# Attention gather in two halves of the TensorE array, with a zero-one product that repeats the parts

## The chip, the core and the metric

The kernel runs on one core of one Trainium2 chip. The metric is device time in microseconds (us) of one execution; several executions are timed and the median is given.

## The reference

One block with two batches of 2048 tokens of width 256, in float32. Only the attention matters here, and of it this:

```python
q, k, v = (split_heads(h @ W + b) for W, b in ...)      # 16 heads of width 16
scores = einsum('bhqd,bhkd->bhqk', q, k) * scale
sparsity = scores.max(-1) - scores.mean(-1)
_, top_idx = top_k(sparsity, U)                         # U = 307 of 2048 queries, per head
q_sel = take_along_axis(q, top_idx[..., None], axis=2)
attn = softmax(einsum('bhud,bhkd->bhuk', q_sel, k) * scale)
out_sel = einsum('bhuk,bhkd->bhud', attn, v)            # scattered back into zeros, then @ Wo
```

The block also has a layer norm ahead of the attention, and after it a second layer norm and a soft mixture of 8 experts.

## The kernel before

The program writes out the order of every engine by hand, with semaphores between the engines. For each batch it makes q, k and v, finds the maximum of the scores of every query (`maxima`, L1080 on VectorE), ranks the queries (`select`), and then runs `attend(b)`, the part that is changed, once for each batch. After both, the experts run.

`attend(b)` goes through 16 heads. To keep float32 accuracy on bf16 matmuls, q and k stand as three bf16 parts each, and a score is a sum of six products of parts. So the stationary and moving operands of a score have 6 * 16 = 96 rows (`TERMS`), of which the query parts are repeated as 0, 0, 0, 1, 1, 2, and 3 more rows with the negated maximum in three parts; 2 further rows carry the query's index. For head h the steps are these.

- **SK and OH** (VectorE, `build` and `onehot`). `SK` holds, for each of the 16 tiles of 128 tokens, 101 columns: the six copies of parts (L1224, six copies), the maximum's parts (L1225) and the index (L1260, once). `OH` is a zero-one matrix, 128 x 307 for each tile, with a one where a token has rank r (L1215, 16 instructions). Both have two buffers.
- **gather** (TensorE, L1666): 16 matmuls, one for each token tile, 101 stationary columns, 307 moving columns, all accumulated in PSUM bank 4. They pick the 307 chosen queries, already turned. They are cut in three pieces (`CUTS`, L1708: tiles 0 to 4, 5 to 10, 11 to 15). For head h the first piece stands at the end of head h - 2 and the other two within head h - 1.
- **take_queries** (ScalarE, L744) copies the 101 rows from PSUM to `QS` in bf16.
- **scores** (TensorE, L1678): 8 steps k = 0 to 7 of two matmuls each, into banks 0 and 1 for even k, 2 and 3 for odd k.
- **exps** (ScalarE, L752): for each step one exponential of 128 x 614 from PSUM to one of four slots of `PX`.
- **values** (TensorE, L1689): 4 steps of four float32 products (each is two matmuls in the trace), each of the four in its own 32-column group of the array.
- **rows** (L1697, three matmuls of one moving column) gives the indices, **turn** (L1704, three transposes) turns the output of the head before, and VectorE (`finish`, L1240 to L1244) divides; POOL scatters the result to DRAM (L609).
- **keys**: SyncE loads the keys of head h + 2 (`attention_keys`, L429) once the scores of head h are done, into one of two buffers `K2S`.

`pe_head` (L1710) sets TensorE's order within a head: for k4 = 0, 1, 2 come scores 2*k4+2 and 2*k4+3, values k4, then for k4 = 0 and 1 a piece of the next head's gather, and for k4 = 2 `rows` and `turn`; then scores 0 and 1 of the next head, values 3, and the first gather piece of the head after the next. `act_head` sets ScalarE's order: exps 0 to 6, take_queries of the next head, exps 7.

The waits that matter: score step k waits on `p_ready` until exps k - 2 has emptied its banks; values k4 waits for exps 2*k4+1; score step 0 of a head waits for `take_queries` of that head; a new gather into bank 4 waits for `take_queries` of the gather before. ScalarE executes strictly in the order written. In the second batch, ScalarE also has a square (L790) after the exps of most heads.

At the start of `attend`, POOL fills pads (`pads`, L580 to L585); the last ones wait for the ranking, and VectorE starts `build` of head 0 only when they are done (L1255).

## Time and profile before

| | us |
|---|---|
| median of 3 runs | 1721.07 |
| the runs | 1720.02 to 1728.72 |
| the profiled execution, its own time | 1707.33 |
| its span, first to last instruction | 1705.2 |

The profile is of one execution, whose own time is 2.1 us above its span and 13.7 us (0.8%) below the median of the runs. The attention stages are about 509 to 637 us and 1016 to 1148 us of the span; the rest is the preparation of each batch (with the maxima) and the experts. In the views, PE is TensorE's matmuls, PEld its weight loads, DVE is VectorE, ACT ScalarE, POOL GpSimd, and SPq SyncE's DMA queue. "a<-b" reads: output a, input b. "issue" as a releaser means that the profile shows nothing that was waited for. A matmul's duration runs from its start to its last result; matmuls overlap, so their pitch is shorter than that.

### The profile page before, as it was taken

How to read it: one execution, taken by the hardware profiler on the slowest of the kernel's cores; microseconds unless marked ns; L12 is line 12 of the kernel's file. 1: busy time of each engine (PE TensorE's matmuls, PEld its weight loads, DVE VectorE, ACT ScalarE, POOL GpSimd, SP SyncE). 2: the span in 40 equal slices, each digit the busy share in tenths (PEclk: the TensorE clock that was granted, in tenths of full speed). 3: DMA queues.
4: the chain of work that ended last, by engine and by line, in shares of the span. 5: the costliest groups of instructions: out<-in, count | busy, mean ns of one | idle time of the engine just before them, and what ended most of it. 6: DMA issues, size and time to landing. Idle time of an engine off the chain costs nothing.

```text
span 1705.2 us, 28768 instructions
## 1 busy us (share of the span) xinstructions
PE 1511.2 (89%) x8650; PEld 846.4 (50%) x8650; DVE 1243.7 (73%) x2937; ACT 1031.6 (60%) x1380; POOL 302.4 (18%) x363
## 2 busy tenths in 40 slices
PE   2779999998859998999999769999899999989999
PEld 1342222222435542222222545543588987469988
DVE  3659999999767858999999777876755452665511
ACT  2338888887736667888888426773333374334364
POOL 1370000000733445000000223442111100011100
PEclk7889999999979999999999879999999999999999
DMA  9441111112331120111112201111034302004410
GB/s 239 178 130 34 41 37 49 44 37 74 121 101 47 52 72 26 48 45 37 41 50 76 62 26 46 52 40 62 13 102 158 126 32 80 0 25 157 157 47 31
DMA packets 91789, 119.25 MB, mean 70 GB/s; under 512 B 21346, under 2 KB 77378, under 8 KB 91204
## 3 DMA queue, kind: packets, MB, share of 16 engines
q1 hardware_dynamic: 88644, 117.73, 22.9%
q0 software_dynamic: 3072, 0.66, 0.4%
q8 instruction: 32, 0.52, 0.1%
q14 instruction: 41, 0.34, 0.1%
HBM read 93.54 MB, written 24.78 MB: 69 GB/s over the span
## 4 chain that ended last, share of the span: by engine, by line
PE 42%; DVE 32%; issue 13%; DMA 5%; ACT 4%; SPq 2%; POOL 1%; PEld 0%; DVEq 0%; ACTq 0%; PEldq 0%; POOLq 0%
DVE work_area L1080 23%; PE psum L1884 6%; PE psum L1822 6%; PE psum L1666 4%; PE psum L1689 4%; PE psum L1765 4%; PE psum L1678 3%; PE psum L1833 3%; PE psum L1842 3%; DVE big_area L1080 2%; PE psum L1525 2%; DMA work_area<-heads_out 2%; PE psum L1874 2%; DVE work_area L1161 1%; ACT big_area L800 1%
## 5 line engine op out<-in xcount | busy, mean ns | idle before, releaser
L1080 DVE CUSTOM_DVE_ANT_0 work_area<-psum,work_area 128x1024 f32<-128x1024 f32 x512 | 589.6, 1220 | 18.4 <-PE psum L1572 14.6
L734 ACT ACTIVATE work_area<-psum 128x1024 f32<-128x1024 f32 x512 | 510.9, 1027 | 88.8 <-DVE big_area L1080 33.1
L1572 PE MATMUL psum<-work_area 96*128 96x512 bf16 x1024 | 312.0, 387 | 47.9 <-DVE big_area L1080 7.6
L1562 PE MATMUL psum<-work_area 96*128 96x512 bf16 x1024 | 309.7, 385 | 12.8 <-DMA work_area<-q_parts 6.8
L752 ACT ACTIVATE work_area<-psum 128x614 f32<-128x614 f32 x256 | 164.1, 681 | 79.4 <-PE psum L1678 78.8
L1572 PEld LDWEIGHTS psum<-work_area 96*128 96x128 bf16 x1024 | 64.4, 98 | 267.3 <-DVE big_area L1080 249.2
L1562 PEld LDWEIGHTS psum<-work_area 96*128 96x128 bf16 x1024 | 89.9, 98 | 161.0 <-ACT work_area L734 57.6
L609 POOL DMA_INDIRECT heads_out<-work_area x96 | 99.1, 1032 | 145.7 <-DVE work_area L1244 124.4
L1215 DVE TENSOR_SCALAR big_area<-iota,rank 128x308 bf16<-128x308 f16 x512 | 122.0, 312 | 0.0
L1822 PE MATMUL psum<-work_area,xn 128*128 128x128 f32 x1024 | 117.3, 275 | 0.0
L1765 PE MATMUL psum<-slots_T,work_area 128*128 128x512 f32 x256 | 116.6, 599 | 0.0
L1884 PE MATMUL psum<-expert_out,work_area 128*128 128x256 f32 x512 | 115.6, 379 | 1.1 <-ACT work_area L865 1.1
L1822 PEld LDWEIGHTS psum<-work_area,xn 128*128 128x128 f32 x1024 | 116.0, 192 | 0.2
L1666 PE MATMUL psum<-big_area,work_area 128*101 128x307 bf16 x512 | 91.4, 315 | 24.4 <-DVE big_area L1215 24.4
L570 POOL CAST negmax_parts<-negmax 128x256 bf16<-128x256 f32 x2 | 1.2, 615 | 577.1 <-DVE sparsity L1148 577.1
L1884 PEld LDWEIGHTS psum<-expert_out,work_area 128*128 128x128 f32 x512 | 95.1, 190 | 13.1 <-ACT work_area L865 1.3
L1666 PEld LDWEIGHTS psum<-big_area,work_area 128*101 128x101 bf16 x512 | 60.7, 133 | 72.5 <-issue 68.6
L1678 PE MATMUL psum<-work_area 99*128 99x307 bf16 x512 | 90.8, 297 | 5.5 <-ACT work_area L752 2.2
L1689 PE MATMUL psum<-work_area 128*32 128x307 f32 x1024 | 93.6, 438 | 0.0
L1421 DVE SCALAR_TENSOR_TENSOR work_area<-psum,rz,x_res 128x256 f32<-128x256 f32 x32 | 15.5, 483 | 98.1 <-PE psum L1884 59.8
L800 ACT ACTIVATE big_area<-psum 128x1024 f32 (+1 forms) x32 | 32.8, 1024 | 88.6 <-PE psum L1765 88.6
L635 POOL TENSOR_TENSOR work_area<-big_area,work_area 128x1024 f32 (+1 forms) x16 | 39.4, 2465 | 205.8 <-PE psum L1826 182.3
(236 smaller groups left out, 1994.4 us busy)
## 6 DMA issues: line engine op xcount, KB each, us to landing
work_area<-in_L_ffn_w_dram SPq DMA_DIRECT2D x32, 1024.0 KB, 5.4
work_area<-q_parts SPq DMA_DIRECT2D x192, 64.0 KB
k_parts<-work_area SPq DMA_DIRECT2D x24, 384.0 KB, 3.2
work_area<-k_parts SPq DMA_DIRECT2D x32, 192.8 KB
q_parts<-work_area SPq DMA_DIRECT2D x16, 384.0 KB, 2.5
big_area<-q_parts SPq DMA_DIRECT2D x16, 384.0 KB, 7.3
work_area<-k_parts SPq DMA_DIRECT2D x32, 192.0 KB
work_area<-k_parts SPq DMA_DIRECT2D x32, 128.5 KB
```

The source lines that it names most:

```text
L734: s.activation(SC[:, t % 4], PS[:, 2 * (n % 2):2 * (n % 2) + 2].rearrange("p a n -> p (a n)"), ACT.Relu).then_inc(relu_done, 1)
L752: s.activation(PX[:, slot, :, 0:U], PS[:, 2 * (k % 2):2 * (k % 2) + 2, 0:U], ACT.Exp, scale=SCALE).then_inc(p_ready, 1)
L1080: v.tensor_tensor_reduce(SC[:, t % 4], PS[:, 4 + 2 * (t % 2):6 + 2 * (t % 2)].rearrange("p a n -> p (a n)"), SC[:, t % 4], 1.0, -3.0e38, A ...
L1215: last = v.tensor_scalar(OH[:, par, t], iota[:], rank[:, t, bass.ds(h, 1)], None, ALU.is_equal)
L1562: last = mm(PS[:, 2 * (n % 2) + k], QS1[par][0:TERMS, t * P:(t + 1) * P], KS[par][0:TERMS, k * 512:(k + 1) * 512], start=True, stop=True)
L1572: last = mm(PS[:, 4 + 2 * (t % 2) + k], QS1[par][0:TERMS, t * P:(t + 1) * P], KS[par][0:TERMS, K1 + k * 512:K1 + (k + 1) * 512], start=Tru ...
L1666: last = mm(PS[0:TERMS + 5, 4, 0:U], SK[:, n % 2, t, 0:TERMS + 5], OH[:, n % 2, t, 0:U], start=(t == 0), stop=(t == NT - 1), skip_group_ch ...
L1678: last = mm(PS[:, 2 * (k % 2) + kk, 0:U], K2S[n % 2][0:TERMS + 3, kt * P:(kt + 1) * P], QS[0:TERMS + 3, n % 2, 0:U], start=True, stop=True)
L1689: last = mm(PS[32 * q:32 * q + 32, 6 - n % 2, 0:U], Vh[:, n % 2, kt], PX[:, kt // 2 % 4, kt % 2, 0:U], start=(kt < 4), stop=(kt >= NT - 4) ...
L1765: last = mm(PS[:, 2 + 2 * par + k], XT[:, par, cc], SNT[:, cc, k * 512:(k + 1) * 512], start=(cc == 0), stop=(cc == DC - 1))
L1822: last = mm(PS[:, cc, 0:P], XN[:, t, cc * P:(cc + 1) * P], E1[:, t], start=(t == 0), stop=(t == NT - 1))
L1884: last = mm(PS[:, 5 - par, 0:D], E2T[:, par, e], EO[:, e], start=(e == 0), stop=(e == E - 1))
```

## The change

The gather's stationary operand `SK` shrinks from 101 used columns to 53 (three parts of 16, three of the maximum, two of the index), held in 64 columns. Even token tiles write to partitions 0 to 63 of bank 4 and odd tiles to partitions 64 to 127. `build` now makes one copy of the parts with 768 elements a partition in place of six with 256. ScalarE copies all 128 rows from PSUM to a new bf16 tile `GQ` (`take_gathered`). One more matmul, `spread`, with the constant zero-one matrix `spread_rows` as its stationary operand, adds the two halves and repeats the parts into the 101 rows, again in bank 4; `take_queries` copies these as before. POOL makes `spread_rows` at the start of the program and clears `SK` in `pads` of each batch. The cuts of the gather become 6, 6 and 4 tiles.

```diff
--- before.py
+++ after.py
@@ -93,6 +93,8 @@
     NG = NT // G
     TERMS = 6 * DH
     UP = U + 1
+    HALF_ROWS = 64
+    PARTS = 3 * DH
     CH = (U + P - 1) // P
     PAIRS = H // 2
     ROUNDS = 16
@@ -153,6 +155,7 @@
         iota = sb("iota", [P, UP], FP16)
         qidx = sb("qidx", [P, NT, 2], BF16)
         hcol = sb("hcol", [P, H])
+        spread_rows = sb("spread_rows", [P, TERMS + 6], BF16)
         idx_rows = sb("idx_rows", [P, 2], BF16)
         stat6 = sb("stat6", [P, NT, 6])
         mv = sb("mean_var", [P, NT, 2])
@@ -207,7 +210,8 @@
         Vh = a.take([2, NT, 32])
         OS = a.take([CH * P])
         QS = a.take([2, UP], BF16)
-        SK = a.take([2, NT, TERMS + 6], BF16)
+        SK = a.take([2, NT, HALF_ROWS], BF16)
+        GQ = a.take([UP], BF16)
         PX = a.take([4, 2, UP])
         OR = a.take([CH, DH + 1])
         ORr = a.take([CH])
@@ -309,6 +313,7 @@
         k2_used = sem("k2_used")
         sk_ready, vh_ready = sem("sk_ready"), sem("vh_ready")
         oh_ready, gathered, idx_ready, idx_used = sem("oh_ready"), sem("gathered"), sem("idx_ready"), sem("idx_used")
+        gq_ready, spread_ready = sem("gathered_copied"), sem("gathered_spread")
         qs_ready, s_ready, p_ready, p_used = sem("qs_ready"), sem("s_ready"), sem("p_ready"), sem("p_used")
         os_ready, oT_ready, oT_used, on_ready = sem("os_ready"), sem("oT_ready"), sem("oT_used"), sem("on_ready")
         pads_ready = sem("pads_ready")
@@ -523,6 +528,16 @@
             g.iota(tmpI[:, UP + 2 * NT:UP + 3 * NT], pattern=[[1, H]], base=0, channel_multiplier=0).then_inc(consts_ready, 1)
             g.memset(steps[:], 0).then_inc(pstep, 1)
             pool.wait_ge(pstep, ps.next())
+            g.memset(spread_rows[:], 0.0).then_inc(pstep, 1)
+            pool.wait_ge(pstep, ps.next())
+            for half in range(2):
+                for at, part in enumerate((0, 0, 0, 1, 1, 2)):
+                    cols = spread_rows[:, at * DH:(at + 1) * DH]
+                    g.affine_select(out=cols, in_=cols, compare_op=ALU.not_equal, fill=1.0, base=-(half * HALF_ROWS + part * DH), pattern=[[-1, DH]], channel_multiplier=1)
+                cols = spread_rows[:, TERMS:TERMS + 5]
+                last = g.affine_select(out=cols, in_=cols, compare_op=ALU.not_equal, fill=1.0, base=-(half * HALF_ROWS + PARTS), pattern=[[-1, 5]], channel_multiplier=1)
+                last.then_inc(pstep, 1)
+                pool.wait_ge(pstep, ps.next())
             for q in range(ROUNDS):
                 for k in range(3):
                     last = g.memset(steps[:, q, k:k + 1], (k + 1) << (29 - 2 * q) if q < 15 else (0, 1, 1)[k])
@@ -581,6 +596,7 @@
                 g.memset(OS, 1.0).then_inc(pads_ready, 1)
                 pool.wait_ge(rank_ready, b + 1)
                 pool.wait_ge(nm_ready, b + 1)
+                g.memset(SK, 0.0)
                 for k in range(2):
                     last = g.memset(K2S[k], 1.0)
                 last.then_inc(pads_ready, 1)
@@ -738,9 +754,14 @@
 
             def attend(b):
 
+                def take_gathered(i, n):
+
+                    act.wait_ge(gathered, b * H + i * 2 + (n + 3))
+                    s.activation(GQ[:, 0:U], PS[:, 4, 0:U], ACT.Identity).then_inc(gq_ready, 1)
+
                 def take_queries(i, par, n):
 
-                    act.wait_ge(gathered, b * H + i * 2 + (n + 3))
+                    act.wait_ge(spread_ready, b * H + i * 2 + (n + 1))
                     s.activation(QS[0:TERMS + 5, par, 0:U], PS[0:TERMS + 5, 4, 0:U], ACT.Identity).then_inc(qs_ready, 1)
 
                 def exps(i, par, gs):
@@ -751,10 +772,14 @@
                         slot = k % 4
                         s.activation(PX[:, slot, :, 0:U], PS[:, 2 * (k % 2):2 * (k % 2) + 2, 0:U], ACT.Exp, scale=SCALE).then_inc(p_ready, 1)
 
+                take_gathered(0, 0)
                 take_queries(0, 0, 0)
 
                 def act_head(i, par, more):
-                    exps(i, par, range(0, 7))
+                    exps(i, par, range(0, 5))
+                    if more:
+                        take_gathered(i, par + 1)
+                    exps(i, par, range(5, 7))
                     if more:
                         take_queries(i, 1 - par, par + 1)
                     exps(i, par, range(7, 8))
@@ -1220,9 +1245,8 @@
                     h = i * 2 + n
                     hd = i * (2 * DH) + n * DH
                     dve.wait_ge(gathered, b * H + i * 2 + (n + 1))
-                    for at, r in enumerate((0, 0, 0, 1, 1, 2)):
-                        v.tensor_copy(SK[:, par, :, at * DH:(at + 1) * DH], QN[:, :, r, bass.ds(hd, DH)])
-                    v.tensor_copy(SK[:, par, :, TERMS:TERMS + 3], NM[:, :, bass.ds(h, 1)].rearrange("p t o r -> p t (o r)")).then_inc(sk_ready, 1)
+                    v.tensor_copy(SK[:, par, :, 0:PARTS].rearrange("p t (r d) -> p t r d", r=3), QN[:, :, :, bass.ds(hd, DH)])
+                    v.tensor_copy(SK[:, par, :, PARTS:PARTS + 3], NM[:, :, bass.ds(h, 1)].rearrange("p t o r -> p t (o r)")).then_inc(sk_ready, 1)
 
                 def indices(i, par, n):
 
@@ -1257,7 +1281,7 @@
                 dve.wait_ge(nm_ready, b + 1)
 
                 for par in range(2):
-                    v.tensor_copy(SK[:, par, :, TERMS + 3:TERMS + 5], qidx[:])
+                    v.tensor_copy(SK[:, par, :, PARTS + 3:PARTS + 5], qidx[:])
                 for par in range(2):
                     build(0, par, par)
                     onehot(0, par, par)
@@ -1663,9 +1687,15 @@
 
                         pe.wait_ge(qs_ready, b * H + i * 2 + n)
                     for t in tiles:
-                        last = mm(PS[0:TERMS + 5, 4, 0:U], SK[:, n % 2, t, 0:TERMS + 5], OH[:, n % 2, t, 0:U], start=(t == 0), stop=(t == NT - 1), skip_group_check=True)
+                        at = t % 2 * HALF_ROWS
+                        last = mm(PS[at:at + HALF_ROWS, 4, 0:U], SK[:, n % 2, t], OH[:, n % 2, t, 0:U], start=(t < 2), stop=(t >= NT - 2), skip_group_check=True)
                     if NT - 1 in tiles:
                         last.then_inc(gathered, 1)
+
+                def spread(i, n):
+
+                    pe.wait_ge(gq_ready, b * H + i * 2 + (n + 1))
+                    mm(PS[0:TERMS + 5, 4, 0:U], spread_rows[:, 0:TERMS + 5], GQ[:, 0:U], start=True, stop=True).then_inc(spread_ready, 1)
 
                 def scores(i, n, k):
                     if k == 0:
@@ -1705,7 +1735,7 @@
                     last.then_inc(oT_ready, 1)
 
 
-                CUTS = (0, 5, 11, NT)
+                CUTS = (0, 6, 12, NT)
 
                 def pe_head(i, n, first, later):
                     for k4 in range(3):
@@ -1716,6 +1746,8 @@
                             gather(i, n + 1, range(CUTS[k4 + 1], CUTS[k4 + 2]))
                         if k4 == 2:
                             rows(i, n)
+                            if later > 0:
+                                spread(i, n + 1)
                             if not first:
                                 turn(i, n - 1)
                     pe.wait_ge(s_ready, b * 128 + i * 16 + (n * 8 + 8))
@@ -1728,6 +1760,7 @@
                         gather(i, n + 2, range(CUTS[0], CUTS[1]))
 
                 gather(0, 0, range(NT))
+                spread(0, 0)
                 scores(0, 0, 0)
                 scores(0, 0, 1)
                 gather(0, 1, range(CUTS[0], CUTS[1]))
```

The names of lines move: the gather is L1691 in the changed kernel, the spread L1698, scores L1708, values L1719, rows L1727, turn L1734, take_gathered L760, take_queries L765 and the exponentials L773. In the first two listings psum and work_area are the memories that hold all the tiles named above.

On TensorE, in the head loop, values 1, the third gather piece and scores 6, before:

```order
L1689 MATMUL psum<-work_area 32x307 [waits p_ready]
L1689 MATMUL psum<-work_area 32x307 x3
L1666 MATMUL psum<-big_area,work_area 101x307 x5
L1675 REGISTER_ALU
L1678 MATMUL psum<-work_area 128x307 [waits p_ready]
L1678 MATMUL psum<-work_area 128x307
```

and in the changed kernel:

```order
L1719 MATMUL psum<-work_area 32x307 [waits p_ready]
L1719 MATMUL psum<-work_area 32x307 x3
L1691 MATMUL psum<-big_area,work_area 64x307 x4
L1705 REGISTER_ALU
L1708 MATMUL psum<-work_area 128x307 [waits p_ready]
L1708 MATMUL psum<-work_area 128x307
```

The piece has 4 matmuls of 64 columns in place of 5 of 101 and stands where it stood.

On TensorE, later in the same head, values 2, rows, turn and the first waits of the next head's scores, before:

```order
L1689 MATMUL psum<-work_area 32x307 [waits p_ready]
L1689 MATMUL psum<-work_area 32x307 x3
L1697 MATMUL psum<-idx_rows,work_area 128x1 [waits idx_used]
L1697 MATMUL psum<-idx_rows,work_area 128x1
L1697 MATMUL psum<-idx_rows,work_area 51x1
L1704 MATMUL psum<-identF,work_area 128x128 [waits oT_used,os_ready]
L1704 MATMUL psum<-identF,work_area 128x128 x2
L1673 REGISTER_ALU [waits s_ready,qs_ready]
L1675 REGISTER_ALU [waits k2_in0]
```

and in the changed kernel:

```order
L1719 MATMUL psum<-work_area 32x307 [waits p_ready]
L1719 MATMUL psum<-work_area 32x307 x3
L1727 MATMUL psum<-idx_rows,work_area 128x1 [waits idx_used]
L1727 MATMUL psum<-idx_rows,work_area 128x1
L1727 MATMUL psum<-idx_rows,work_area 51x1
L1698 MATMUL psum<-work_area,spread_rows 101x307 [waits gathered_copied]
L1734 MATMUL psum<-identF,work_area 128x128 [waits oT_used,os_ready]
L1734 MATMUL psum<-identF,work_area 128x128 x2
L1703 REGISTER_ALU [waits s_ready,qs_ready]
L1705 REGISTER_ALU [waits k2_in0]
```

One matmul of 101 columns, which waits for ScalarE's first copy, stands between rows and turn; the scores of the next head still wait for `qs_ready`, which the second copy sets.

On ScalarE, the first head of the first batch and the beginning of the second (L752 and L773 are the exponentials, L744 and L765 take_queries, L760 take_gathered), before:

```order
L752 ACT_TABLE_LOAD [waits p_used]
L752 ACTIVATE work_area<-psum 128x2x307 [waits s_ready]
L752 ACTIVATE work_area<-psum 128x2x307 [waits p_used,s_ready] x6
L744 ACTIVATE work_area<-psum 101x307 [waits gathered]
L752 ACTIVATE work_area<-psum 128x2x307 [waits p_used,s_ready] x8
```

and in the changed kernel:

```order
L773 ACT_TABLE_LOAD [waits p_used]
L773 ACTIVATE work_area<-psum 128x2x307 [waits s_ready]
L773 ACTIVATE work_area<-psum 128x2x307 [waits p_used,s_ready] x4
L760 ACTIVATE work_area<-psum 128x307 [waits gathered]
L773 ACTIVATE work_area<-psum 128x2x307 [waits p_used,s_ready] x2
L765 ACTIVATE work_area<-psum 101x307 [waits gathered_spread]
L773 ACTIVATE work_area<-psum 128x2x307 [waits p_used,s_ready] x6
L760 ACTIVATE work_area<-psum 128x307 [waits gathered]
```

Between exponentials 4 and 5 of a head there is now the copy that waits for the whole gather of the next head, and the old copy now waits for the spread.

## Rows read from the trace of the kernel before

**Rows 1.** The page of the profile: span, and busy time of each engine.
```profile
span 1705.2 us, 28768 instructions
...
PE 1511.2 (89%) x8650; PEld 846.4 (50%) x8650; DVE 1243.7 (73%) x2937; ACT 1031.6 (60%) x1380; POOL 302.4 (18%) x363
```

**Rows 2.** Busy time of each engine in the attention stages of both batches.
```profile
509.00:637.00 128.00, 125.40 (x1097) 67.92 (x1098) 88.76 (x395) 86.65 (x145) 49.15 (x56) 1.00 0.21 57
1016.00:1148.00 132.00, 129.34 (x1097) 69.32 (x1101) 101.82 (x448) 93.34 (x172) 49.88 (x56) 0.97 0.16 46
```

**Rows 3.** Chain of waits inside one head: start us, us, what.
```profile
561.02 0.92 PE psum L1666 x6
...
562.47 0.66 PE psum L1689 x8
563.12 0.79 PE psum L1666 x5
563.92 0.53 PE psum L1678 x4
...
565.10 0.25 PE psum L1697 x3
...
568.98 0.92 PE psum L1666 x6
```

**Rows 4.** Timeline, one head: start us, us, engine, line, operation [idle before <-releaser].
```profile
562.25 1.25 ACT L752 ACTIVATE work_area<-psum 128x614 f32<-128x614 f32 x2 [0.85 <-PE psum L1678]
...
563.05 0.86 PE L1666 MATMUL psum<-big_area,work_area 128*101 128x307 bf16 x5
...
563.75 0.69 PE L1678 MATMUL psum<-work_area 99*128 99x307 bf16 x4
...
564.37 0.72 PE L1689 MATMUL psum<-work_area 128*32 128x307 f32 x8
...
564.79 0.42 ACT L744 ACTIVATE work_area<-psum 101x307 bf16<-101x307 f32 x1
...
565.03 0.32 PE L1697 MATMUL psum<-idx_rows,work_area 101*128 101x1 bf16 x3
565.10 0.69 ACT L752 ACTIVATE work_area<-psum 128x614 f32<-128x614 f32 x1
...
565.66 0.69 PE L1678 MATMUL psum<-work_area 99*128 99x307 bf16 x4
```

**Rows 5.** All matmuls of the gather, L1666: duration ns min/median/max.
```profile
L1666 PE MATMUL psum<-big_area,work_area x512: 292/294/498, 504.6 to 1139.4; 128*101 128x307 bf16 x171
```

**Rows 6.** Groups by form, 509 to 637 us: the exponentials.
```profile
L752 ACT ACTIVATE work_area<-psum 128x614 f32<-128x614 f32 x128 | 82.0, 681 | 40.8 <-PE psum L1678 40.7
```

**Rows 7.** Who waited for whom, 509 to 637 us: us in total, times, longest.
```profile
PEld psum L1666 <- issue: 21.9, 44, 0.5
...
PEld psum L1689 <- issue: 16.2, 64, 0.3
```

**Rows 8.** Chain of waits, start of the first batch's attention.
```profile
495.69 3.53 POOL work_area L585 x2
...
499.60 1.25 DVE work_area L1224 x6
...
504.63 4.25 PE psum L1666 x16
```

**Rows 9.** Chain of waits, key loads late in the first batch's attention.
```profile
614.09 7.60 DMA work_area<-k_parts
...
621.81 0.69 PE psum L1678 x4
```

**Rows 10.** Chain of waits, a key load in the second batch's attention.
```profile
1053.68 7.57 DMA work_area<-k_parts
1061.37 0.69 PE psum L1678 x4
```

**Rows 11.** Timeline of POOL, first part of the program.
```profile
56.12 1.16 POOL L541 TENSOR_TENSOR work_area<-work_area 128x512 bf16<-128x512 f32 x1 [48.70 <-DVE work_area L1027]
```

## The prediction

> **What bounds the kernel now.** I read the page first [rows 1]: TensorE (PE) is busy 89% of a span of 1705.2 us. That is a mean, so I went to the two attention stages, the only ones that the change touches: there PE is busy 125.4 of 128 us and 129.3 of 132 us, ScalarE (ACT) 86.7 and 93.3 us, VectorE 88.8 and 101.8 us [rows 2]. The chain of waits within a head is PE from end to end, and repeats every 568.98 - 561.02 = 7.96 us [rows 3]: two gather pieces of five products, one of six, four values steps of 0.66, four pairs of score steps of 0.53, rows 0.25, turn. So PE's work sets the head's period today, and what the change takes from the gather seems a gain at once. The timeline [rows 4] is the view that decides, since it shows how close ACT runs behind PE: exps 4 starts at 562.25, exps 5 0.58 later (the 1.25 of the row is a pair of 0.68 each, overlapping by 0.1 [rows 4, 6]), both before the third gather piece starts at 563.05.
>
> **The prices, from the rows.** A six-product gather piece takes 0.92 and a five-product one 0.79, so one product costs 0.13 and a piece 0.14 beside its products [rows 3]. Scores start at 563.75 and the values after them at 564.37: 0.62 for four products of 0.13, so 0.10 is lost where the array goes from 128 to 32 columns [rows 4]. In that loss PE's weight loads stand idle too, 0.25 us before each of 64 values steps and 0.5 before each of 44 gather pieces and what follows values [rows 7]. Between a gather piece and the scores behind it there is no such loss today. The Trainium skill, TensorEngine Tiling (Array Packing), section Key Properties, says that a change of tiling mode drains TensorE; the rows agree, and by that rule the change has three more such points a head.
>
> **Gather.** The values steps already run four 32-column groups side by side: eight matmuls in 0.66, where eight in turn at 0.13 would take at least 1.04 [rows 3]. I take pairs of 64 columns to run the same way, one pair for the price of one product, 0.13. A new piece of three pairs is then 0.14 + 0.39 = 0.53, plus 0.10 to go back to 128 columns: 0.63. Against 0.79 and 0.92 that saves 0.16 on the first and 0.29 on the second piece, 0.45. The third, of two pairs, is costed below. Bounds: nothing lost at the way back (0.10 less a piece), and for a pair 0.26, the two products in turn as now. I take 0.13, since the values rows are the nearest.
>
> **ACT's new place in the order.** Here the change costs more than it saves. ACT takes its work strictly in order. Between exps 4 and exps 5 it now has the first copy, which waits for the last product of the third gather piece, and this product comes behind values 1. Count from T = 563.05, the start of that piece.
> - The last pair starts at T + 0.17 (two pairs: 0.04 of the piece's cost and 0.13). Its result is there 0.29 later [rows 5] and ACT starts 0.04 after (564.79 + 0.31 = 565.10 is how soon the next ACT instruction follows such a copy [rows 4]). Copy at T + 0.50, exps 5 at T + 0.81.
> - Exps 5 takes 0.68 [rows 6], and with 0.05 for the signal scores 7 start at T + 1.54, since they write the banks that exps 5 reads. Today they start at 563.75 + 0.26 = T + 0.96. This is the stall of about 0.9 us: PE has been ready since some T + 0.66.
> - From scores 7 to rows takes today 565.03 - 564.01 = 1.02 [rows 4], rows 0.25 [rows 3]. The spread starts at T + 2.81, its result is with ACT after 0.33, at T + 3.14; then take_queries, exps 7 0.31 later, 0.68 long, 0.05: score step 1 of the next head, whose banks exps 7 empties, starts at T + 4.18. Today it starts at 565.66 + 0.26 = T + 2.87. Step 0, which waits for take_queries, is done by then.
> - So this half of the head is 1.31 longer, and everything before and after it follows. The third piece's own saving and the spread's 0.13 are inside this path.
>
> Per head: +1.31 - 0.45 = +0.86, a period of 8.8 us in place of 7.96. Fifteen heads a batch have a gather behind them, 30 in all: **+25.8 us**. Nothing hides it: PE waits for ACT and ACT for PE in turn, about 1.5 us a head in which neither has work. The squares on ACT in the second batch stand after exps 7 and ahead of exps 0, whose result is wanted a values step and a gather piece later, so they stay covered.
>
> **Other parts.**
> - The key loads. The load for head h + 2 is issued when the scores of head h are done and takes 7.6 us [rows 9, 10]; now and then it ends last, and the four score products take 0.69 in place of 0.53 [rows 9, 10]. With 0.9 us more a head it no longer does. I take -1 us for all of them, bounds 0 and -1.5.
> - The start of each batch. POOL clears SK after the ranking, ahead of the two fills of 3.53 us that everything waits for [rows 8]: one more of that size, +1.77. VectorE's build, 1.25 for six copies of 256 elements [rows 8], becomes one of 768, the size of three: -0.6. The first gather runs at the lower TensorE clock, 4.25 for 16 products, 0.26 each [rows 8, 5]: eight steps less, -2.1. Then one copy with its signals and the spread: 0.46 + 0.05 + 0.5 (a product's 498 ns at that clock [rows 5]), +1.0. Sum 0; bounds -1 and +3 a batch, the upper if less PE work keeps the clock at 1.2 GHz longer or if the first key load, also 1.77 later, ends last.
> - Build in the loop gets shorter and is not waited for: VectorE has over 30 us idle in each stage [rows 2]. The zero-one matrix is made while POOL would be idle 48.7 us [rows 11]: nothing.
>
> **The sum.** 25.8 - 1 + 0 = +24.8. On the profiled execution, 1705.2 of span and 2.1 around it, 1707.3, that is 1732.1. The median of the runs is 13.7 higher; on it the forecast is 1721.1 + 24.8 = **1745.9 us**, 1.4% slower. About 0.5%, 9 us, is what a measurement of this kernel can tell from no change.
>
> **Rivals.**
> 1. *The gain comes through* (faster). If exps 5 were not held up, PE's own work would be the period: 0.45 saved on two pieces, 0.79 - (0.14 + 0.26 + 0.10) = 0.29 on the third, 0.13 spent on the spread, -0.61 a head, 30 heads: -18 us, 1703. For it: PE is the whole chain today. The key loads, at times last even now [rows 9, 10], might take a part of it back. Against it: the order of ACT's program. Exps 4 ends at 562.93, the copy can't start before 563.55, and exps 5, which starts at 562.83 today, stands behind it. It decides if the gather is finished when exps 4 ends, or if exps 5 has slack that I don't see. The Trainium skill, TensorEngine Tiling, section Theoretical Speedup, gives up to 2x where a dimension is 64 or less; that rule alone, on 16 products of 0.13, is this rival. Its section PSUM Bottleneck warns that the copies out of PSUM may then bind, which is how I read this case, though here it is their order and not their sum. Chance 0.08.
> 2. *The halves don't run side by side* (the change doesn't do what it says). 64-column products in turn cost 0.13 more a pair, all eight pairs of a head on the path: +1.04, 30 heads +31, in all +56: 1777. For it: no product of 64 columns is in the trace, and 64 columns of weights per product must be loaded twice as often. Against it: the 32-column groups of the values. Chance 0.12.
> 3. *The waits overlap better* (no change). If the signals are quicker and the way back from the gather is free, 0.3 less a head and path, and half of the stall is taken up by slack elsewhere, the total is within 9 us: about 1725. Chance 0.06.
>
> **How the numbers follow.** The forecast has 0.74. Slower by over 0.5% is it and rival 2, 0.86; same 0.06; faster 0.08. The range: the lower end takes no loss on the way back (-0.2 a head, -6), -1.5 for the keys and -1 at the starts, 1738, and lets the runs fall somewhat towards the profiled execution, which lies 13.7 below the median: 1730. The upper end takes a pair at 0.20, halfway between its bounds (0.07 on eight pairs, 30 heads, +17), and +5 at the starts: 1768. Rival 2 in full and rival 1 stay outside, 0.2 together.
>
> **What would show it.** Right: PE waits for exps (L773) at scores 7 and again at the next head's score steps 0 and 1, some 0.9 and 0.3 and 0.3 us; ACT waits about 0.7 for the gather at the first copy and 1.2 for the spread at the second; rows products 8.8 apart; values-like starts a few ns apart within a pair of gather products, pairs 0.13 apart; three fills of 1.8 in the pads. Wrong: a period of 7.4 with PE without waits (rival 1), or gather products 0.13 apart one by one and a period near 9.9 (rival 2).

## The result, and the profile after the change

| | us |
|---|---|
| kernel before, median of 4 runs beside the change | 1724.89 (1720.02 to 1730.22) |
| changed kernel, median of 4 runs | 1762.41 (1761.82 to 1766.97) |
| ratio | 1.0226, 95% interval 1.02 to 1.0252 |
| profiled execution of the change, its own time | 1766.97 |

The change costs 37.5 us, 2.3%. The forecast was +24.8, 1745.9 us, with a range of 1730 to 1768: its sign was right, and its size was 12.7 us short. (Against 1745.9 itself the result is 16.5 us above: 3.8 of that is the median of the kernel before, which moved from 1721.1 to 1724.9 with a fourth run.)

The page of the changed kernel, span and engines (before: [rows 1]):

```profile
span 1765.2 us, 28711 instructions
...
PE 1526.1 (86%) x8682; PEld 808.1 (46%) x8682; DVE 1226.5 (69%) x2777; ACT 1043.9 (59%) x1412; POOL 309.7 (18%) x380
```

The attention stages in the windows view (start:end, us, then busy time of PE, PEld, DVE, ACT and POOL, then the granted clock, DMA share and GB/s):

```profile
512.00:671.00 159.00, 137.29 (x1107) 50.42 (x1105) 79.75 (x321) 90.76 (x159) 49.65 (x56) 0.88 0.17 47
1049.50:1204.00 154.50, 131.04 (x1106) 48.46 (x1104) 93.20 (x371) 97.49 (x185) 50.80 (x56) 0.93 0.14 39
```

From the first exponential to the last, the stages take 158.9 and 154.6 us; in the profile of before they take 125.8 and 130.2. PE, which hardly waited in [rows 2], is now idle for 22 of 159 us. There is a second thing that I did not expect: the granted clock of the stages is 0.88 and 0.93 in place of 1.00 and 0.97. TensorE ran at 1.2 GHz for 36.4 and 21.4 us of them, before for 0 and 6.9.

The timeline of the changed kernel, the middle of the third head (as [rows 4]; L1708 is scores, L1719 values, L1691 gather, L773 the exponentials, L760 the first copy):

```profile
534.98 0.70 PE L1708 MATMUL psum<-work_area 99*128 99x307 bf16 x4
535.49 1.16 POOL L625 DMA_INDIRECT heads_out<-work_area  x1 [0.30 <-issue]
...
535.61 0.72 PE L1719 MATMUL psum<-work_area 128*32 128x307 f32 x8
...
536.26 0.45 PE L1691 MATMUL psum<-big_area,work_area 128*64 128x307 bf16 x4
536.65 0.43 POOL L617 COPY work_area<-big_area 128x272 f32 x1
537.01 0.68 ACT L773 ACTIVATE work_area<-psum 128x614 f32<-128x614 f32 x1 [2.10 <-PE psum L1708]
537.59 0.42 ACT L760 ACTIVATE work_area<-psum 128x307 bf16<-128x307 f32 x1
...
537.75 0.43 PE L1708 MATMUL psum<-work_area 99*128 99x307 bf16 x2 [1.04 <-ACT work_area L773]
```

Read it from the ACT line at 537.01, which is exps 4. Its scores are the first two products of the PE line at 534.98 and end at 535.41, yet exps 4 starts 1.6 us later, after 2.10 us of idle time. Nothing on ACT stands in its way. The forecast stall is there as well (the first copy L760 between exps 4 and exps 5), but this wait comes ahead of it. The rows products of neighbouring heads are 8.87 us apart for the first two heads of each batch, against a forecast of 8.8, and then 9.5 to 11.2 (the last full interval of the second batch is 8.87 again). Exps 4 starts 0.04 after its scores in heads 0 and 1 of both batches, and 1.4 to 1.6 after in most of the others (1.60 in head 2, 1.51 in head 5, 1.54 in head 9); where it is less late, in heads 4, 8, 11 and 14 of the first batch, the interval that it stands in ran for 5.0 to 5.6 us at 1.2 GHz and took 10.5 to 10.8.

So two losses need a cause: exps 4 is late, and the clock falls. In the trace's semaphore events the first can be told apart from a slow TensorE. In the same head the signals of scores 4 and 5, of values 1 and of the last gather product all arrive between 536.99 and 537.18, though their products end between 535.41 and 536.71. TensorE works on time, and its signals come late and together.

### The profile page after: what moved, and what is told of

The parts are those of the page before. It is cut to its first block, busy times and chain, and to the rows that moved or that the text cites. A ratio compares the mean times of both kernels' runs of the same rounds, so it can differ in the third digit from the quotient of the medians.

```text
span 1765.2 us, 28711 instructions
## 1 busy us (share of the span) xinstructions
PE 1526.1 (86%) x8682; PEld 808.1 (46%) x8682; DVE 1226.5 (69%) x2777; ACT 1043.9 (59%) x1412; POOL 309.7 (18%) x380
## 4 chain that ended last, share of the span: by engine, by line
PE 44%; DVE 31%; issue 13%; ACT 6%; DMA 3%; POOL 1%; SPq 1%; DVEq 0%; ACTq 0%; POOLq 0%
DVE work_area L1105 22%; PE psum L1708 6%; PE psum L1917 6%; PE psum L1855 6%; PE psum L1719 4%; PE psum L1798 4%; PE psum L1866 3%; PE psum L1875 2%; PE psum L1691 2%; PE psum L1549 2%; DVE big_area L1105 2%; DMA work_area<-heads_out 2%; ACT work_area L773 2%; PE psum L1907 1%; ACT big_area L825 1%
## 5 line engine op out<-in xcount | busy, mean ns | idle before, releaser
L773 ACT ACTIVATE work_area<-psum 128x614 f32<-128x614 f32 x256 | 164.4, 684 | 80.0 <-PE psum L1708 58.6
L1708 PE MATMUL psum<-work_area 99*128 99x307 bf16 x512 | 107.8, 320 | 46.4 <-ACT work_area L773 34.6
L1719 PE MATMUL psum<-work_area 128*32 128x307 f32 x1024 | 101.1, 469 | 0.7 <-ACT work_area L773 0.7
L1708 PEld LDWEIGHTS psum<-work_area 99*128 99x128 bf16 x512 | 36.4, 101 | 109.7 <-ACT work_area L773 72.5
L1691 PE MATMUL psum<-big_area,work_area 128*64 128x307 bf16 x512 | 56.8, 331 | 26.8 <-DVE big_area L1240 26.8
L1264 DVE TENSOR_REDUCE work_area<-psum 128x51 f32<-128x204 f32 x32 | 11.9, 372 | 94.7 <-PE psum L1734 94.1
```

What stands on the lines that cost most here:

```text
L773: s.activation(PX[:, slot, :, 0:U], PS[:, 2 * (k % 2):2 * (k % 2) + 2, 0:U], ACT.Exp, scale=SCALE).then_inc(p_ready, 1)
L1708: last = mm(PS[:, 2 * (k % 2) + kk, 0:U], K2S[n % 2][0:TERMS + 3, kt * P:(kt + 1) * P], QS[0:TERMS + 3, n % 2, 0:U], start=True, stop=True)
L1719: last = mm(PS[32 * q:32 * q + 32, 6 - n % 2, 0:U], Vh[:, n % 2, kt], PX[:, kt // 2 % 4, kt % 2, 0:U], start=(kt < 4), stop=(kt >= NT - 4) ...
```

## The experiments

All of them are edits of the changed kernel or of the kernel before. The first two sets of four kernels ran on one chip, on which the kernel before takes 1728.6 and 1725.6; the later runs came to two other chips, on which it takes 1705.1 and 1708.3. That difference turned out to matter. The chip of the result itself is not on record. By its kernel before (1724.9) and by its late exps 4 it behaves as the first of the three, and it is counted as that one below.

One thing is needed to read the intervals. The first of a batch has no `turn` in it, since head 0 has no head before it. In the kernel before it is 7.88, and 7.96 with the `turn`.

### 1. Move the copies back in ScalarE's order

```diff
-                    exps(i, par, range(0, 5))
+                    exps(i, par, range(0, 7))
                     if more:
                         take_gathered(i, par + 1)
-                    exps(i, par, range(5, 7))
+                    exps(i, par, range(7, 8))
                     if more:
                         take_queries(i, 1 - par, par + 1)
-                    exps(i, par, range(7, 8))
```

> The changed kernel with ScalarE's order altered alone: exps 0 to 6, first copy, exps 7, second copy. My theory (the loss is the place of the two copies in ScalarE's order): neither exps 5 nor exps 7 waits for the gather or the spread any more; the heads come 7.7 us apart, 0.25 less than in the kernel before, and the time is about 7 us (0.4%) below the kernel before, some 45 us below the changed kernel. Rival A (the array's changes between 64, 32 and 128 columns, or the extra matmul, cost it): order matters little, heads stay 8.9 or more apart, the time stays at least 20 us above the kernel before. Rival B (the late exps 4 in the heads of TensorE's loop, 0.65 us a head, is a thing of the loop by itself and not a consequence of the stall): heads of 7.7 outside the loop and 8.4 in it, about 8 us above the kernel before. Clock: if its falls come from the waits, the granted clock of the attention stages is back at 0.97 or more.

Measured: 1748.57 us, ratio 1.0127 (1.0091 to 1.0163). The time is not what the theory says: 20 us above the kernel before and not 7 below, which by itself would suit Rival A. The intervals decide. The first interval of each batch is 7.68, as the theory says, and the last full interval of the second batch, with a `turn`, 7.81. Nearly all those between are 9.2 to 9.5. Rival A falls with these two: with the copies out of the way, halves, mode changes and spread together cost less than what they save. But the saving is smaller than 7.68 makes it look. Against the kernel before it is 0.20 without a `turn` and about 0.12 with one (7.84 in experiments 6 and 8, against 7.96). The extra 1.5 us a head is the lateness, larger than Rival B had it, and here it is not hidden by any other wait. TensorE was at 1.2 GHz for 13.7 and 10.6 us of the stages, in place of 36.4 and 21.4. Below, this order of ScalarE is called the late order. The timeline of this kernel, one late head (L1707 is scores, L1718 values):

```profile
570.75 0.70 PE L1707 MATMUL psum<-work_area 99*128 99x307 bf16 x4
571.05 1.17 POOL L625 DMA_INDIRECT heads_out<-work_area  x1 [0.31 <-issue]
...
572.22 0.44 POOL L617 COPY work_area<-big_area 128x272 f32 x1
572.87 1.90 ACT L773 ACTIVATE work_area<-psum 128x614 f32<-128x614 f32 x3 [2.18 <-PE psum L1707]
```

and its exps 4 and 5 in head 1, in time (the gap ahead of them is only TensorE's work):

```profile
526.08 1.26 ACT L773 ACTIVATE work_area<-psum 128x614 f32<-128x614 f32 x2 [0.54 <-PE psum L1707]
```

In the late head values 0 ends at 570.31 and its semaphore rises at 572.75, 2.44 later. Scores 4 and 5 (end 571.19 and 571.45) follow at 572.84 and 572.89, values 1 (572.10) at 572.98. After that everything is prompt again. POOL was issuing an indirect DMA, one of the three by which a head's output is scattered, at 569.77 to 570.75, when values 0 ended.

### 2. Half of the move

```diff
-                    exps(i, par, range(0, 5))
+                    exps(i, par, range(0, 6))
                     if more:
                         take_gathered(i, par + 1)
-                    exps(i, par, range(5, 7))
+                    exps(i, par, range(6, 7))
```

> The changed kernel with ScalarE's order exps 0 to 5, first copy, exps 6, second copy, exps 7: half of what the late order does. My theory: exps 5 is free, exps 7 still waits for the spread; heads 7.9 to 8.0 apart, the time equal to the kernel before within 5 us. Rival A (the matmuls and their mode changes cost it): at least 20 us above. Rival B (lateness of the loop by itself): about 16 us above the kernel before.

Measured: 1744.27 us, 1.0108 (1.0069 to 1.0148). The time is 15.7 us above the kernel before, not within 5 of it; that is the size of Rival B. The first interval is 7.96 in both batches and the last full one of the second batch too, as the theory has it; nearly all others are 9.2 to 9.3. TensorE was at 1.2 GHz for only 5.2 and 7.1 us of the stages. The lateness, once nothing covers it, brings both orders to the same period.

### 3. Write out TensorE's loop

```diff
-                with pe.Fori(1, PAIRS - 1) as i:
+                for i in range(1, PAIRS - 1):
                     for n in range(2):
                         pe_head(i, n, False, 2)
```

> The changed kernel with TensorE's loop over heads 2 to 13 written out, nothing else. Theory for the part that I did not forecast (exps 4 starts 1.5 us late in the heads of the loop, since TensorE's queue in the loop holds its register instructions and semaphore waits behind it): all full-clock heads come 8.87 us apart, as heads 0, 1 and 14 do now, exps 4 starts 0.04 after scores 4, and the time falls by 0.65 on 24 heads, 16 us, to about 1.3% above the kernel before. Rival (the lateness comes from where the heads stand against each other, not from the loop): no change, 2.2% above.

Measured: 1758.16 us, 1.0183 (1.0148 to 1.0219). The heads stay at 9.4 to 9.6 where the clock is full, and exps 4 is 1.3 to 1.6 late in most heads from head 2 on, as in the change. My first theory of the lateness, that TensorE's loop with its register instructions holds the signals, is wrong.

### 4. The chain without the halves

The kernel before with its full gather, and in it the first copy, a spread through an identity, and the second copy, where the changed kernel has them.

```diff
+                    s.activation(QS[0:TERMS + 5, n % 2, 0:U], PS[0:TERMS + 5, 4, 0:U], ACT.Identity).then_inc(gq_ready, 1)
...
+                    mm(PS[0:TERMS + 5, 4, 0:U], identB[0:TERMS + 5, 0:TERMS + 5], QS[0:TERMS + 5, n % 2, 0:U], start=True, stop=True).then_inc(spread_ready, 1)
...
-                    exps(i, par, range(0, 7))
+                    exps(i, par, range(0, 5))
+                    if more:
+                        take_gathered(i, par + 1)
+                    exps(i, par, range(5, 7))
```

> The kernel before with its full gather of 101 columns and its cuts of 5, 6 and 5 tiles, but with the first copy, a matmul with an identity of 101 rows as the spread, and the second copy, in the places of the changed kernel. It has the added chain and no halves. My theory: the first copy waits longer (piece of five full products, 0.2 later), no piece is cheaper; heads 9.9 us apart, 58 us above the kernel before without a lateness in the loop, up to 75 with it; so the chain alone costs more than the whole change, and the halves give back some 20 to 30. Rival A (the halves' mode changes are what costs): heads below 8.6, less than 20 us above the kernel before.

Measured: 1770.36 us, 1.0245 (1.0204 to 1.0287): +42, against 58 expected. The heads are 9.74 apart (9.9 expected), all through the first batch. By the times alone the chain costs as much as the whole change (+42 and +37.5, with intervals that overlap); the period tells more. It is 9.74 in place of 7.96, so the chain is the loss, and the halves give 9.74 - 8.87 = 0.87 of it back (8.87 is the change in a head without late signals). The stages of this profile take 152 and 158 us in place of the 125.8 and 130.2 of the profile before, 54 us more. That the measured difference is only 42 is a first sign that on this chip the kernel before takes longer than its profile. Exps 4 is late here too, by about 1.0, but nobody pays for it: exps 5 stands behind the first copy, which waits for the gather, until 1.8 after its scores in any case. And the clock stays at its upper level throughout the first batch. The windows view of this kernel:

```profile
513.00:665.00 152.00, 134.71 (x1100) 65.00 (x1099) 85.80 (x383) 91.09 (x159) 49.41 (x56) 1.00 0.18 48
```

### 5. The halves without the chain

```diff
-                    act.wait_ge(spread_ready, b * H + i * 2 + (n + 1))
-                    s.activation(QS[0:TERMS + 5, par, 0:U], PS[0:TERMS + 5, 4, 0:U], ACT.Identity).then_inc(qs_ready, 1)
+                    act.wait_ge(gathered, b * H + i * 2 + (n + 3))
+                    s.activation(QS[:, par, 0:U], PS[:, 4, 0:U], ACT.Identity).then_inc(qs_ready, 1)
...
-                            if later > 0:
-                                spread(i, n + 1)
```

ScalarE has the order of the kernel before in it, exps 0 to 6, the one copy, exps 7.

> The halves alone: gather in pairs of 64 columns, no first copy, no spread, one copy of all 128 rows as in the kernel before; the exponentials run with scale 0, so that the attention weights are all equal (the output is not the reference's), the indices stay right. In the earlier runs the heads 2 to 13 lost a further 1.6 us, since TensorE's signals (values 0, scores 4 and 5, values 1, last gather product) all came late and together, some 2.4 us after values 0 ended. Theory A (the halves gain their 0.74 a head, and the late signals belong to the added chain or to its timing): heads 7.2 apart, 22 us below the kernel before. Theory B (the late signals are independent of the chain: scatters of POOL overlap values 0 in a bad phase): heads 0 and 14 near 7.2, the others 8.5 or more, the time at or above the kernel before.

Measured: 1726.23 us, 1.0006 (0.9987 to 1.0024): no difference. The first interval is 7.10 in both batches (7.2 expected) against 7.88 in the kernel before, so the halves do save their 0.8 a head on TensorE. The others are mostly 9.1 to 9.6 in the first batch and 7.2 to 9.4 in the second: there exps 4 is late again, by up to 2.1 us. Theory B holds. The lateness needs neither copy nor spread.

### 6. Take the scatters away

```diff
-                    for j in range(CH):
-                        w = min(P, U - j * P)
-                        g.indirect_dma_start(
-                            out=heads_out[b], out_offset=bass.IndirectOffsetOnAxis(ap=IDX[0:w, par, j:j + 1], axis=0),
-                            in_=ON[0:w, par, j], in_offset=None).then_inc(scattered[par], 16)
+                    pool.sem_inc(scattered[par], CH * 16)
```

With the late order:

> The changed kernel with the late order of ScalarE (exps 0 to 6, first copy, exps 7, second copy) and without POOL's scatter DMAs of the attention heads (POOL raises the semaphore itself; the attention's rows stay zero, the output is not the reference's). Theory B (TensorE's signals are held up while POOL issues the indirect DMAs, when these overlap values 0): all heads 7.7 apart, exps 4 starts 0.04 after scores 4, 48 us less in the two stages than with the scatters, about 1% below the kernel before. Rival (the scatters have no part in it): heads stay at 9.2 to 9.3, the time 1.2% above the kernel before.

Measured: 1714.51 us, 0.9918 (0.9878 to 0.9958). No exps 4 is late. Nearly all intervals are 7.68 to 8.5 in place of 9.2 to 9.5: 7.68 is the first of each batch, with a `turn` they are 7.84 at the least, and their mean in the first batch is 8.02 and not the 7.7 expected. Experiment 8 shows what holds it there. With the order of the change:

> The changed kernel without POOL's scatter DMAs of the attention heads, nothing else. Theory B: heads 8.87 apart throughout (the stall that I forecast, and no more), 20 us less than the changed kernel, 1.0 to 1.2% above the kernel before; if the clock's falls in the stages come from the forecast stall alone, they remain (0.95), if from the late signals, the clock is at 0.97 or more. Rival (the scatters have no part in it): 9.55 and more, 2.2% above.

Measured: 1736.46 us, 1.0067 (1.0044 to 1.009). In the first batch all of the 14 intervals are 8.86 or 8.87, the 8.8 of the forecast, no exps 4 is late, and TensorE is at 1.2 GHz for 5.1 and 9.6 us of the stages in place of 36.4 and 21.4. So the late signals need the scatters. Without these the changed kernel takes 1762.4 - 1736.5 = 26 us less on this chip (20 expected), nearly all of it in the heads, and experiment 9 has heads of 8.86 with the scatters in place, so it is the lateness that costs there and not the scatters' own work. Most of the clock's falls go with it: the forecast stall alone, as long as it is, leaves the clock nearly alone. The rival (the scatters have no part in it) is out. The time is only 0.67% above the kernel before, less than the 1.0 to 1.2% expected; the kernel before still has its scatters.

### 7. The numbers of the semaphores

```diff
-        gq_ready, spread_ready = sem("gathered_copied"), sem("gathered_spread")
...
         y_out = [sem(f"y_out{i}") for i in range(2)]
+        gq_ready, spread_ready = sem("gathered_copied"), sem("gathered_spread")
```

> The late order of ScalarE again, with the two new semaphores allocated behind all others, so that every other semaphore has the number that it has in the kernel before. Rival C (it is the shift of the semaphores' numbers that makes the signals late, as the kernels with the chain all have it and the kernel before has not): heads 7.7 apart, 0.4% below the kernel before. Theory B: no change, heads 9.3, 1.2% above.

Measured: 1747.12 us, 1.0128 (1.0094 to 1.0161), heads of 9.2 to 9.5: rival C is out.

### 8. Hold the scatters

Two kernels, the late order and the kernel before, with this on POOL:

```diff
+                        if paced:
+                            pool.wait_ge(p_used, b * 64 + i * 8 + ((n + 2) * 4 + 1 + j))
+                            pool.sem_inc(pool_held, 1)
                         g.indirect_dma_start(
```

> The changed kernel with the late order of ScalarE and with each of the three scatter DMAs of a head (heads 0 to 13) held on POOL until values 0, 1 and 2 of the head two later are done, so that no indirect DMA is being issued when values 0 ends. In the runs so far exps 4 was late in almost all heads in which the issue of one spanned the end of values 0, and in time in nearly all others. If this overlap is the cause: exps 4 starts 0.04 after scores 4 in all heads, the heads are 7.7 to 7.9 apart as without scatters, and the time is 0.6 to 1% below the kernel before, which would beat both kernels. If any overlap of an indirect DMA with the end of a signalled product does it: the lateness moves to another step and the heads stay near 9.3.

> The kernel before with the same hold on its scatters, nothing else. Its profile shows no late signal, so by that nothing changes: within 5 us of the kernel before. But its profiled execution was 13 to 18 us faster than the median of its other executions; if those have late signals in some heads that the profiled one lacks, this kernel takes them away: 10 to 15 us (0.6 to 0.9%) below the kernel before.

> The kernel before once more, for a second profile: its first one (1707) lies well below the median of its executions (1725). If the median has late signals in part of its heads, a profiled execution near 1725 shows exps 4 more than 0.5 late in some of them; if the difference is elsewhere (the clock, the key loads, the experts), all heads are 8.0 apart and the difference stands outside the attention stages.

These three ran on another chip, where the kernel before has a median of 1705.11 in 9 runs. Measured: late order 1717.22, 1.0066 (1.0045 to 1.0086); before with held scatters 1712.33, 1.0045 (1.003 to 1.006); before again 1705.35. Both held kernels are slower than the kernel before, so both expectations failed; why the hold costs the kernel before its 7 us is not explained (in the profiles 3.8 of them stand between the two attention stages). No signal is late in any of the three, and so they say nothing on whether holding helps: the kernel before, with nothing held, has none either on this chip. The question put to the third run is not answered, since it did not meet the chip on which the median is 1725.

The pair does answer another one. Both have held scatters and no late signals, and the late order is still 4.9 us slower, though its intervals are 7.84 at the least, against 7.96 (7.68 and 7.89 for the first). Its waits of PE in the first batch (waiting line, what for: us in total, times, longest), and from its chain of waits two loads of the keys:

```profile
PE psum L1710 <- DMA work_area<-k_parts: 6.0, 8, 1.0
```

```profile
552.66 7.65 DMA work_area<-k_parts
560.30 0.12 issue
560.42 0.70 PE psum L1710 x4
...
569.21 7.34 DMA work_area<-k_parts
576.55 0.12 issue
576.67 0.70 PE psum L1710 x4
```

and the same waits in the second profile of the kernel before:

```profile
PE psum L1678 <- DMA work_area<-k_parts: 0.4, 2, 0.2
```

Two heads after a key load that ends last, the next one ends last again, 16.25 us later, 8.12 a head. The first 14 intervals of the first batch have a mean of 8.04 in the late order, of 8.02 in the held kernel before and of 8.02 in the kernel before; in the second batch the two held kernels both have 8.28. What TensorE and ScalarE save, the waits for the loads into two buffers take back. That reading rests on the waits and the chain; no run here changed the key loads. With the heads even, the 4.9 us stand elsewhere: in the two profiles 2.4 of them in the first stage, most of that in its last interval (10.32 against 8.88), and 3.2 after the second.

### 9. One batch held, one not

```diff
+                        if paced and b == 1:
+                            pool.wait_ge(p_used, b * 64 + i * 8 + ((n + 2) * 4 + 1 + j))
+                            pool.sem_inc(pool_held, 1)
```

> The changed kernel with its own order of ScalarE, with the scatters held in the second batch only; the first batch is the changed kernel as it is. The kernel before has a median of 1725 on the chip of the first two sets and of 1705 on that of the last, at the same granted clock, so late signals may belong to a chip. On a chip where before takes 1725: batch 0 shows exps 4 late by 1.5 and heads of 9.6 and more, as in the profile of the change; if holding the scatters cures it, batch 1 has heads of 8.87 and no exps 4 late; if not, both batches look alike. The time is then some 12 us below the changed kernel's, +1.4%, or else +2.2%. On a chip where before takes 1705: if the lateness belongs to the chip, batch 0 has heads of 8.87 with no exps 4 late although nothing is held there, and the time is 25 to 30 us above the kernel before, 1.6%, which is the forecast; if it belongs to the change, batch 0 has heads of 9.6 there too.

Measured, on a third chip: 1737.96 us beside 1708.3, ratio 1.017 (1.0145 to 1.0195), +29.7 us. In both batches exps 4 starts 0.04 after its scores in every head, and the intervals are 8.86, 13 of 14 in the second batch and all 14 in the first, in which nothing is held. The scatters overlap the end of values 0 just as they do in the profile of the result: in head 3 the three DMAs are issued from 2.00 to 0.99, from 0.68 before to 0.31 after, and from 0.61 to 1.78 after that end there, and within 0.01 of these times here. There exps 4 is 1.56 late, here 0.04. So the lateness needs the scatters (experiment 6) and did not show on this chip, nor on the second one with the kernel before; where it is absent, the change costs what its own chain costs. The 29.7 us are those of a kernel with its second batch held, and in experiment 8 a hold had a cost of its own. The change just as it was made was not timed on a chip without late signals. The windows of this kernel:

```profile
511.00:651.00 140.00, 123.28 (x1106) 46.64 (x1104) 79.48 (x321) 91.85 (x159) 49.41 (x56) 0.98 0.19 52
1030.00:1172.00 142.00, 123.20 (x1103) 46.30 (x1101) 91.90 (x372) 97.64 (x185) 49.61 (x56) 0.98 0.15 43
```

## Why the prediction was right, and where it was short

**The stall.** The last kernel shows the mechanism without the disturbance, in its first batch, which is the change as it was made. Its timeline, one head (L1694 is gather, L1711 scores, L1701 the spread, L763 and L768 the copies, L776 the exponentials):

```profile
561.11 0.45 PE L1694 MATMUL psum<-big_area,work_area 128*64 128x307 bf16 x4
...
561.60 0.43 ACT L763 ACTIVATE work_area<-psum 128x307 bf16<-128x307 f32 x1 [0.62 <-PE psum L1694]
561.92 1.25 ACT L776 ACTIVATE work_area<-psum 128x614 f32<-128x614 f32 x2
...
562.66 0.43 PE L1711 MATMUL psum<-work_area 99*128 99x307 bf16 x2 [0.73 <-ACT work_area L776]
...
563.93 0.34 PE L1701 MATMUL psum<-work_area,spread_rows 128*101 128x307 bf16 x1
...
564.30 0.43 ACT L768 ACTIVATE work_area<-psum 101x307 bf16<-101x307 f32 x1 [1.12 <-PE psum L1701]
...
565.35 0.11 PEld L1711 LDWEIGHTS psum<-work_area 99*128 99x128 bf16 x2 [0.29 <-ACT work_area L776]
```

| step, from T = 561.11 | forecast | measured |
|---|---|---|
| first copy starts | 0.50 | 0.49 |
| exps 5 | 0.81 | 0.81 |
| scores 7 | 1.54 | 1.55 |
| spread | 2.81 | 2.82 |
| take_queries | 3.14 | 3.19 |
| score step 1 of the next head | 4.18 | 4.24 |
| period | 8.8 | 8.86 |

The waits that were to show it, in the first batch of this kernel:

```profile
PE psum L1711 <- ACT work_area L776: 11.0, 15, 0.7
...
PE psum L1711 <- ACT work_area L768: 5.5, 15, 0.5
...
ACT work_area L768 <- PE psum L1701: 16.8, 15, 1.1
...
ACT work_area L763 <- PE psum L1694: 9.3, 15, 0.6
```

Fifteen of each: 0.73 at scores 7 (0.9 forecast), 0.36 at step 0 (0.3), 0.62 and 1.12 on ACT (0.7 and 1.2).

**The gather.** Two products of a pair start 2 to 4 ns apart and the pairs 0.13, and the way back to 128 columns costs 0.10. A pair costs what one product did, as the chain of waits of the last kernel has it:

```profile
559.38 0.51 PE psum L1694 x6
...
561.18 0.38 PE psum L1694 x4
```

That is 0.51 for three pairs against 0.92 for six products [rows 3]. Rival 2 is out. The 0.87 that experiment 4 gives for the halves is also about what the steps make of it: 0.79 + 0.92 - 2 x 0.51 less 0.10 twice for the way back, 0.49 for the first two pieces (0.45 forecast), and for the third 0.79 less 0.38, 0.41. Of the two sections weighed in the forecast, the Trainium skill, TensorEngine Tiling (Array Packing), section Theoretical Speedup, holds for the pair by this trace. Its section PSUM Bottleneck, which says that the copy out of PSUM may become the bottleneck after a 4x speedup of TensorE, points at the right engine but not at the mechanism: ACT is busy only 92 of 140 us, and it is the place of the copies, not their sum, that binds.

**Starts of the batches.** The chain of waits of the changed kernel (as [rows 8]):

```profile
496.94 1.77 POOL work_area L599
498.71 3.50 POOL work_area L601 x2
...
502.58 0.49 DVE work_area L1248
...
507.07 2.28 PE psum L1691 x16
```

The fill is 1.77 as forecast, the build 0.49 in place of 1.25 (-0.8, forecast -0.6), the first gather 2.28 in place of 4.25 (-2.0, forecast -2.1).

**Key loads.** They no longer end last in the heads at 8.86, as forecast: no wait for them is among PE's in either batch of the last kernel.

**The sum.** Against the second profile of the kernel before, span 1703.2 (on another chip), the last kernel's 1736.1 is 32.9 longer: -0.8 up to the first exponential, +12.7 and +14.2 in the stages, +1.4 between them, +5.4 in the experts. The forecast had +24.8 for the stages, their starts and the keys together. The stages, the start and the stretch between give 27.5, the stages alone 26.9. The 5.4 after the last head was not forecast, and no run here explains it; TensorE is at 1.2 GHz for 20.5 us there, against 17.1. By the medians on its own chip this kernel, with its second batch held, costs 29.7, 4.9 over the forecast.

**What was short.** On the chip of the result the missing term was not the stall. The step "Per head: +1.31 - 0.45 = +0.86, a period of 8.8 us" left out that TensorE's signals can come late, and in the upper bound the clock stood at the starts alone ("+3 a batch"), while it fell within the stages. Neither is in the profile of the kernel before, which I read as the kernel on every chip. There was a hint in the numbers, and I passed over it: the profiled execution was 13.7 us below the median and 12.7 below the fastest of the others. I took the median as the same execution plus a constant. With what the runs show now, that profile has the time of the other two chips (1705 and 1708 against its 1707), not that of the chip on which the medians were taken. The difference of some 18 us is not the clock: at a granted clock of 0.965 the runs of the kernel before take 1720 to 1726 on the first chip and 1704 to 1707 on the other two. It is likely that the kernel before loses it to late signals of its own, but that is only argued: no profile of it was taken on that chip.

**What was luck.** The mechanism and its price were right, but that the result on that chip fell inside 1730 to 1768 was in part luck. The late signals cost the changed kernel 26 there, and the kernel before is some 18 slower there than on the other chips; only the difference of the two shows (29.7 + 26 - 18 = 37.7, against 37.5 measured). And the upper end was made of a dearer pair of products (+17) and dearer starts (+5). Neither came true: pairs cost 0.13, and the starts came out near 0. What filled the room was a loss that the forecast did not name.

**Rival 1** (the gain comes through) was given 0.08. With the copies moved out of the way TensorE's period is 7.84 (7.68 where there is no `turn`), so the stall was a choice of place and not a must; but it is not the 7.4 of that rival. Even then the mean is 8.04, by the waits for the key loads, which that rival named and priced too low ("might take a part of it back"). Of the two changed kernels that ran where signals are prompt, neither beats the kernel before, and both had scatters held; the late order with nothing held did not run there. The late order without scatters is 0.8% below it on the first chip, but it leaves work out.

## What to carry to other kernels

When a piece of work is made shorter on the busiest engine and a copy is added on the second, draw the second engine's order and ask what stands behind the copy's wait. Here 0.9 us a head came from one instruction that waited ahead of exps 5, and it could be read from six rows to 0.06 us. If the profiled execution is a per cent away from the median, find out first what separates them, before its rows are used for the median. And look for the loop of buffers next in line: the copies moved out of the way made the engines' own period 0.12 shorter, and the mean head stayed at 8.0 while TensorE waited for the key loads.

## What the runs showed of the hardware

- On one of three chips, signals of TensorE (semaphore events of finished products) came late and together, while POOL issued indirect DMAs: values 0's by 2.44 us in the head shown, exps 4 by up to 2.1 after its scores (experiment 5). The products were on time. Without these DMAs, on the same chip, the heads were 8.86 apart as they are on a chip with prompt signals. On two other chips no exps 4 was late with DMAs that nothing held (the kernel before on one, the first batch of the changed kernel on the other, there in the same places to 0.01 us). Most late heads had an indirect DMA under way at the end of values 0, but so do the kernels on the other chips, so the overlap is not enough as a condition. What in the chip does it stays open, and so does whether holding the DMAs back helps there: that was tried only on chips without the lateness.
- The clock: with the forecast stall alone (0.7 and 0.4 us of waits a head) TensorE was at 1.2 GHz for 4.2 and 4.2 us of the stages. With stall and late signals it was 36.4 and 21.4. With late signals and the copies half out of the way (experiment 2) it was 5.2 and 7.1. With the chain alone, at a longer period of 9.74, it was 0 in the first batch.
- Two products of 64 columns side by side, both with 307 moving columns, start 2 to 4 ns apart and cost 0.13 together, one product's price. The first gather at 1.2 GHz took 2.28 for eight pairs.
